# Small router products between key products, a narrower first wait for the query product, the sum's low part in four slices, and the shift row ahead of two stores

## The chip, the cores and the metric

One Trainium2 chip, one of its cores. The metric is the device time of one execution in microseconds. The kernel is written by hand: each engine (TensorE or PE, VectorE or DVE, ScalarE or ACT, GpSimd or POOL, and SyncE or SP, which only issues DMAs) has its own list of instructions in program order, and semaphores join the lists. An instruction that waits holds up everything behind it on its engine.

## The reference

Inputs are x (8 x 512 tokens x 512) and a context of 8 x 120 x 512. The first half is cross-attention with 16 heads of 32; all eight "experts" see the same attention output and their mean is taken, so that only the sum of the eight matrices We matters. The second half is a top-1 router over 8 experts, of which each takes 100 tokens at most, with one common matrix.

```
q = layernorm(x) @ Wq.T + bq;  k = ctx @ Wk.T + bk;  v = ctx @ Wv.T + bv
attn = softmax(q k.T / sqrt(32)) v                      # by head
x = x + tanh(g_xattn) * (mean_e(attn @ We[e].T + be[e]) @ Wo.T + bo)
h = layernorm(x); best = argmax(h @ w_gate)             # first 100 tokens of each expert
x = x + tanh(g_ffn) * gate * (h @ w_expert + b_expert)  # for those tokens
```

## The kernel before, in words

Every large product is split in two float16 parts, high and low, and made of three products (high by high, high by low, low by high), so each operand has a `_hi` and a `_lo` tile: ACT writes the high part out of a PSUM bank, then DVE writes the low part from the same bank and the high part.

**The prologue** is a list of 52 units, written down by `unit` and its callers. A unit is one PSUM bank: what PE does in it (`pe`), which semaphore counts PE waits for first (`needs`, and `free`: the evacuation of the unit eight places earlier, whose bank it takes), and what ACT and DVE do to empty it. PE, ACT and DVE each run through the list in its order. A unit's "done" is a count on `s_pa` (ACT) and on `s_pv` (DVE), and as both count along the list, a unit that waits for another also waits for all before that one. The units are: turning Wk (4 units), the biases, turning the context (one unit for each of 8 batch rows), four key units for batch rows 0 to 3 (`k_units(0)`), turning Wv (4), four key units for rows 4 to 7 (`k_units(1)`), turning Wq (4), the router's small units, turning Wo (4), and then the value products `v_unit(0)` to `v_unit(7)` with a few small units and the four units `x_unit` (which turn the first normalised x) between them. Key and value units have twelve products each. The small units are

- `gate_rows_unit` (L475): eight transposes of 4 x 128 out of `wg_rows`; it waits for `s_const`, which counts three loads, the last of them `bv_bc`; DVE copies it into `wg`;
- `be_unit` (L445): four products with the summed biases of the experts; it waits for `s_const` too;
- `gates_unit` (L469): one product that spreads the two gates, followed by the tanh on ACT;
- `gate_mean_unit` (L458): four products with `wg`; it needs DVE's copy of `wg`. After its evacuation DVE also makes `route_hi` and `route_lo` (L1299, L1302).

Beside the units ACT issues the DMAs that store the keys in a DRAM scratch (`store_k`, L1067; 12 for each half): those of the first half behind the unit four places after the last key unit of that half, those of the second half ahead of the unit `wogT`. DVE takes the statistics of the first x (`stats1`, `moments1`) behind the key unit ("k", 1, 2), and POOL makes 1/std from them and then adds up the eight matrices We in seven additions (`sum_we`), each of which waits for a load. SP has issued all loads in order; a load of We waits for the tile it overwrites.

**The first query product.** After the units PE goes through `run([-1], ...)`: the four query tiles of batch row 0 (`q_tile`, L892: `q_begin` and `q_end`), the router's product with x (`route_x`, L838), the products for the softmax maxima (`max_scores`, L896), and between them six late units (`mix_bias`, the four `("mix", k)` that multiply Wo with the sum of We, and `gateT`), which share three banks. `q_begin` calls `first_units_over` (L588) ahead of the first query product: all ACT and DVE evacuations of the 52 units, and all stores of the keys. The mix units need `sum_hi` (ACT, L1108) and `sum_lo` (DVE, `sum_low`, L1315: one instruction for 128 x 2048).

**Batch rows.** Then `run(range(0, B - 1), ...)` runs each batch row r with parts of rows r + 1 and r - 1 between its own. `scores(b, 0)` (L779) waits for `q_stack`, in which three parts are made by DMAs and the last partition holds the row of maxima, the "shift row": DVE `maxima`, PE `max_turn`, ACT `shift_row`, then a DMA on SP's queue into `q_stack`. On SP that DMA stands in the loop over r at L735 to L739; for r = 6 (B - 2) two stores of output tiles stand ahead of it:

```
                    if r == B - 2:
                        store_tiles(r, (0, 1))
                    e.wait_ge(s_sh, r + 2)
                    load(q_stack[3 * DK:STACK, :, :, :]..., shift[:, :], s_rsh)
```

The last batch row (7) has its own order with the experts' rows between.

Of the kernel before, what the change touches and what calls it, by code (L numbers as in the profile page):

```python
# [45 lines left out]
ALU = mybir.AluOpType  # L46
# [33 lines left out]
def build(nc, x, ctx, g_xattn, g_ffn, Wq, bq, Wk, bk, Wv, bv, We, be, Wo, bo, w_gate, w_expert, b_expert, out):  # L80
# [7 lines left out]
    with ExitStack() as st:  # L88
# [270 lines left out]
        def needs_of(*names):  # L359
            return [w for n in names for w in made[n]]  # L360
# [55 lines left out]
                ins = e.matmul(out_, a(pa, k), b(pb_, k), start=(i == 0), stop=(i == len(steps) - 1))  # L416
            return ins

        def k_units(half):
            lo_b, hi_b = half * HALF, (half + 1) * HALF  # L420
            for g in range(NK):
                def pe(e, b, g=g):
                    return products3(e, b[:, 0:HALF * SK],
                                     lambda p, k: (wkT_hi, wkT_lo)[p][:, k, g * P:(g + 1) * P],
                                     lambda p, k: (ctxT_hi, ctxT_lo)[p][:, k, lo_b * SK:hi_b * SK])
                unit(("k", half, g), pe,
                     needs_of(*[("wkT", k) for k in range(NK)], *[("ctxT", b_) for b_ in range(lo_b, hi_b)], "bias"),
                     act=lambda e, b, g=g: e.activation(
                         k_hi[:, lo_b:hi_b, g, :], b[:, 0:HALF * SK].rearrange("p (b s) -> p b s", s=SK),
                         ACT.Identity, bias=bias_cols[:, NK + g:NK + g + 1]),  # L430
                     dve=lambda e, b, g=g: e.scalar_tensor_tensor(
                         out=k_lo[:, lo_b:hi_b, g, :], in0=b[:, 0:HALF * SK].rearrange("p (b s) -> p b s", s=SK),
                         scalar=bias_cols[:, NK + g:NK + g + 1], in1=k_hi[:, lo_b:hi_b, g, :],
                         op0=ALU.add, op1=ALU.subtract))

        def v_unit(b_):
            def pe(e, b):
# [70 lines left out]
        def mix_units():  # L508
            def three(e, b, left, right):
                steps = [(o, i, j) for o in range(NK) for i, j in ((0, 0), (0, 1), (1, 0))]  # L510
                for n, (o, i, j) in enumerate(steps):
                    ins = e.matmul(b[:, :], left(i, o), right[j][:, o, :], start=(n == 0), stop=(n == len(steps) - 1))  # L512
                return ins

            wo = (woT_hi, woT_lo)
            unit("mix_bias", lambda e, b: three(e, b, lambda i, o: (be_hi, be_lo)[i][:, o:o + 1].to_broadcast([P, P]), wo),
                 needs_of("be_col", *[("woT", k) for k in range(NK)]) + [(s_bo, 16)],
                 dve=lambda e, b: e.scalar_tensor_tensor(out=mix_bias[:, :], in0=b[:, :],
                                                         scalar=1.0 / (BIAS_SCALE * OUT_SCALE), in1=bo_bc[:, :],
                                                         op0=ALU.mult, op1=ALU.add))  # L520
            for k in range(NK):
                def pe(e, b, k=k):
                    return three(e, b, lambda i, o: (sum_hi, sum_lo)[i][:, o, k * P:(k + 1) * P], wo)

                unit(("mix", k), pe, needs_of(*[("woT", o) for o in range(NK)]) + [(s_sumh, 1), (s_suml, 1)]
                     + ([(s_qhi, 3 + k), (s_qlo, 3 + k)] if k < 2 else []),
                     act=lambda e, b, k=k: e.activation(mixT_hi[:, k, :], b, ACT.Copy, scale=mix_scale[:, 0:1]),
                     dve=lambda e, b, k=k: e.scalar_tensor_tensor(
                         out=mixT_lo[:, k, :], in0=b, scalar=mix_scale[:, 0:1], in1=mixT_hi[:, k, :],
                         op0=ALU.mult, op1=ALU.subtract))  # L530
# [16 lines left out]
             dve=lambda e, b: e.tensor_tensor(bias_cols[:, :], b[:, 0:3 * NK], bias_unit[:, :], ALU.mult))  # L547
        for b_ in range(HALF + 2):
            ctx_unit(b_)
        k_units(0)  # L550
        for b_ in range(HALF + 2, B):
            ctx_unit(b_)
        weight_units("wvT", pair=(mixT_hi, mixT_lo), scale=V_SCALE)
        k_units(1)
        weight_units("wqT", pair=(wqT_hi, wqT_lo), scale=QK_SCALE)
        gate_rows_unit()
        be_unit()
        gates_unit()
        gate_mean_unit()
        weight_units("woT", pair=(woT_hi, woT_lo), scale=OUT_SCALE)  # L560
        v_unit(0)
        gate_out_rows_unit()
# [9 lines left out]
        N_FIRST = len(units)  # L572
        FIRST_ACT = sum(u["act"] is not None for u in units)
        FIRST_DVE = sum(u["dve"] is not None for u in units)
        late.append(N_FIRST)
        mix_units()
        gate_units()
# [64 lines left out]
        def _(e):  # L642
# [63 lines left out]
            for r in range(-1, B):  # L706
# [19 lines left out]
                if ok(r + 1):  # L726
                    e.wait_ge(s_sc, 4 * (r + 1))
                    e.wait_ge(s_qhi, 4 * (r + 2))
                    for part, src in ((0, q_hi), (2, q_hi), (1, q_lo)):
                        if part == 1:  # L730
                            e.wait_ge(s_qlo, 4 * (r + 2))
                        for j in range(HJ):
                            if (part, j) not in ACT_STACKS:
                                load(q_stack[part * DK:(part + 1) * DK, j, :, :], src[j * DK:(j + 1) * DK, :, :], s_rq)
                    if r == B - 2:  # L735
                        store_tiles(r, (0, 1))
                    e.wait_ge(s_sh, r + 2)
                    load(q_stack[3 * DK:STACK, :, :, :].rearrange("o j g s -> o (j g) s"),
                         shift[:, :], s_rsh)  # L739
                if ok(r + 2):  # L740
                    turn_x(r + 2)
            e.wait_ge(s_sc, 4 * B)
# [10 lines left out]
        def _(e):  # L753
# [82 lines left out]
                return ins  # L836

            def route_x(b, _):  # L838
                e.wait_ge(s_xth, 16 * b)
                e.wait_ge(s_xtl, 16 * b)  # L840
                if ok(b - 2):
# [25 lines left out]
            def q_begin(b, g):  # L867
                if g == 0:
                    if b == 0:
                        first_units_over(e)  # L870
                    e.wait_ge(s_xth, 16 * b)
                    e.wait_ge(s_xtl, 16 * b)
                    if ok(b - 2):
# [358 lines left out]
        def _(e):  # L1232
# [62 lines left out]
            for i in range(N_FIRST):  # L1295
                prepare(0, i)
                if units[i]["done"] == made["wg_mean"]:
# [4 lines left out]
                    e.scalar_tensor_tensor(out=route_lo[:, 0, :, 0:NE], in0=wgc[:, :, NE:2 * NE], scalar=GATE_SCALE,  # L1302
                                           in1=route_hi[:, 0, :, 0:NE], op0=ALU.mult,
                                           op1=ALU.subtract).then_inc(s_route, 1)
                if units[i]["done"] == made[("k", 1, 2)]:
                    for t in range(NT):
                        stats1(0, t)
                    moments1(0, 0)
# [3 lines left out]
                    moments1(1, 0)  # L1312
            first_units_over(e)

            def sum_low(_, __):  # L1315
                e.wait_ge(s_sumh, 1)
                e.scalar_tensor_tensor(out=sum_lo[:, :, :], in0=w_sum[:, :, :], scalar=SUM_SCALE, in1=sum_hi[:, :, :],
                                       op0=ALU.mult, op1=ALU.subtract).then_inc(s_suml, 1)

            def scale_bias(_, __):  # L1320
                e.wait_ge(*made["gates"][0])
# [155 lines left out]
            def add_table(b, _):  # L1477
# [5 lines left out]

            late_unit = lambda i: (prepare, 1, N_FIRST + i)
            run([-1], [
                (q_low, 1, 0), (maxima, 1, 0), (q_low, 1, 1), (sum_low, 1, 0), (q_low, 1, 2), (maxima, 1, 1),
                (q_low, 1, 3),
                (maxima, 1, 2), late_unit(0), (maxima, 1, 3),
                (normalise1, 2, 0), (normalise1, 2, 1), (normalise1, 2, 2), (normalise1, 2, 3),
                late_unit(1), (x_lo, 2, 0), (x_lo, 2, 1), late_unit(2), (x_lo, 2, 2), (x_lo, 2, 3), late_unit(3),  # L1490
                (scale_bias, 1, 0), late_unit(4),
            ])
# [276 lines left out]
```

## Time and profile before

| | us |
|---|---|
| three runs, median (lowest to highest) | 453.32 (452.45 to 453.39) |
| the profiled execution, its own time | 453.2 |
| its span, first to last instruction | 451.4 |
| PE busy | 427.3 (95%) |
| DVE busy | 343.1 (76%) |
| ACT busy | 224.3 (50%) |
| POOL busy | 161.9 (36%) |
| mean granted TensorE clock | 0.989 |

The span is 1.8 us shorter than the execution's time. Stretches on the timeline below are in us from the first instruction. A PE product's listed duration goes to its modelled end; in a run of products the distance of two starts is what each takes. The bracket behind a row is the idle time of the engine ahead of it, and what ended it. The granted clock is 1.00 at 2.4 GHz and 0.50 at 1.2 GHz. By time the prologue's units run to 75.8, batch row 0's own start to about 109, and each batch row takes 38.8 after that (the shift row is loaded at 298.31 and at 337.08).

### The profile page before, as it was taken

Reading aid. Unit: us, or ns where it says so; the run is one execution under the profiler, and the core shown is the slowest. Engines: PE = TensorE matmul, PEld = TensorE weight load, DVE = VectorE, ACT = ScalarE, POOL = GpSimd, SP = SyncE. Lnnn points to the kernel's source line nnn. Section 1 sums busy time; section 2 is a strip of 40 time slices with the busy share of each in tenths; the row PEclk is TensorE's granted clock in tenths of the full one; section 3 lists DMA queues with packets and bytes.
Section 4 is the critical chain, followed back from the end, with each engine's and each line's share of the span. In section 5 each row is a group of like instructions: output and inputs, shape, how many; then the busy total and the mean of one; then the engine's idle time right before and its main releaser. Section 6 shows DMA issues by size and latency. Waiting matters only on the chain.

```text
span 451.4 us, 8251 instructions
## 1 busy us (share of the span) xinstructions
PE 427.3 (95%) x2903; PEld 197.3 (44%) x2903; DVE 343.1 (76%) x671; ACT 224.3 (50%) x278; POOL 161.9 (36%) x149
## 2 busy tenths in 40 slices
PE   5998999899999999999999999999999998969996
PEld 4457565343344434534443443453444344324442
DVE  5438426786498889879889987988995598769983
ACT  4333321465753856476374656728456473657200
POOL 1005899206025308324430820523171062170460
PEclk9998899999999999999999999999999999989999
DMA  8997692058006724940780492188058016041683
GB/s 228 321 390 278 252 399 72 1 119 216 5 1 146 194 94 104 166 164 12 165 249 8 106 231 98 39 138 251 5 119 220 0 44 165 25 129 44 105 184 111
DMA packets 64842, 63.15 MB, mean 140 GB/s; under 512 B 41217, under 2 KB 44429, under 8 KB 64803
## 3 DMA queue, kind: packets, MB, share of 16 engines
q1 hardware_dynamic: 59691, 56.19, 46.8%
q0 software_dynamic: 1632, 3.49, 2.8%
q10 hardware_dynamic: 3480, 2.96, 1.9%
q8 instruction: 24, 0.39, 0.4%
q14 instruction: 15, 0.12, 0.1%
HBM read 29.59 MB, written 12.98 MB: 94 GB/s over the span
## 4 chain that ended last, share of the span: by engine, by line
PE 67%; DVE 12%; issue 10%; ACT 6%; DMA 3%; SPq 2%; DVEq 0%; ACTq 0%; POOLq 0%
PE ps L755 49%; PE ps L416 9%; ACT probs L1062 4%; DVE neg_max L1382 3%; DVE attn L1342 3%; PE ps L512 3%; PE ps L378 3%; DVE q_lo L1376 2%; SPq L644 2%; DMA raw<-in_L_xattn_Wk_dram 1%; DVE rden_both L1337 1%; DMA rows<-out_dram,row_ix 1%; PE ps L535 1%; PE ps L486 1%; DMA q_stack<-shift 1%
## 5 line engine op out<-in xcount | busy, mean ns | idle before, releaser
L1062 ACT ACTIVATE probs<-ps 120x2048 f32<-120x2048 f32 x32 | 60.1, 1879 | 43.7 <-PE ps L755 43.7
L1692 POOL TENSOR_TENSOR attn_lo<-attn,attn_hi 128x512 f16<-128x512 f32 x28 | 31.6, 1160 | 114.5 <-ACT attn_hi L1062 114.5
L1382 DVE TENSOR_REDUCE neg_max<-ps 128x16 f32<-128x1920 f32 x32 | 68.5, 2141 | 1.9 <-PE ps L755 1.9
L755 PE MATMUL ps<-xnT_hi,wqT_hi 128*128 128x512 f16 x128 | 48.6, 380 | 1.0 <-issue 0.9
L755 PE MATMUL ps<-mixT_hi,attn_hi 128*128 128x512 f16 x128 | 48.6, 380 | 0.0
L755 PE MATMUL ps<-mixT_lo,attn_hi 128*128 128x512 f16 x128 | 48.5, 379 | 0.0
L755 PE MATMUL ps<-xnT_lo,wqT_hi 128*128 128x512 f16 x128 | 48.5, 379 | 0.0
L1637 POOL TENSOR_SCALAR veps<-mv 128x4 f32<-128x4 f32 (+1 forms) x17 | 4.5, 265 | 121.5 <-DVE mv L1271 84.7
L1700 POOL TENSOR_TENSOR xb<-xb,mix_bias 128x512 f32<-128x512 f32 x32 | 39.6, 1269 | 22.5 <-DVE cb_col L1325 22.5
L1062 ACT ACTIVATE q_hi<-ps,bias_cols 128x512 f16<-128x512 f32 x32 | 21.9, 684 | 40.1 <-PE ps L755 40.1
L1376 DVE SCALAR_TENSOR_TENSOR q_lo<-ps,bias_cols,q_hi 128x512 f16<-128x512 f32 x32 | 23.8, 744 | 20.7 <-ACT q_hi L1062 20.7
L755 PE MATMUL ps<-q_stack,k_stack 97*120 97x512 f16 x128 | 33.9, 387 | 3.1 <-DMA q_stack<-shift 1.7
L755 PE MATMUL ps<-probs,den_sel 120*32 120x512 f32 x256 | 34.1, 605 | 0.1
L755 PE MATMUL ps<-probs,v_all 120*32 120x512 f32 x256 | 33.3, 592 | 0.7 <-ACT attn L1062 0.7
L755 PE MATMUL ps<-mixT_hi,attn_lo 128*128 128x512 f16 x128 | 33.0, 380 | 0.0
L755 PE MATMUL ps<-xnT_hi,wqT_lo 128*128 128x512 f16 x128 | 32.9, 379 | 0.0
L1062 ACT ACTIVATE q_stack<-q_hi 32x2048 f16<-32x2048 f16 x16 | 30.5, 1908 | 0.5
L1348 DVE SCALAR_TENSOR_TENSOR xb<-ps,xb 128x512 f32<-128x512 f32 x32 | 21.9, 685 | 11.2 <-PE ps L755 11.2
L1332 DVE RECIPROCAL rden<-ps 128x512 f32<-128x512 f32 x8 | 26.9, 3357 | 3.9 <-PE ps L755 3.9
L1062 ACT ACTIVATE attn<-ps 128x512 f32<-128x512 f32 x32 | 19.0, 594 | 17.4 <-PE ps L755 17.3
L1062 ACT ACTIVATE attn_hi<-attn 128x512 f16<-128x512 f32 x32 | 19.6, 630 | 12.5 <-DVE attn L1342 12.5
L755 PEld LDWEIGHTS ps<-q_stack,k_stack 97*120 97x120 f16 x128 | 15.0, 133 | 20.7 <-ACT probs L1062 7.9
(248 smaller groups left out, 822.8 us busy)
## 6 DMA issues: line engine op xcount, KB each, us to landing
xb<-in_x_dram SPq DMA_DIRECT2D x8, 1024.0 KB, 6.3
q_stack<-q_hi SPq DMA_DIRECT2D x48, 128.0 KB
out_dram<-xb SPq DMA_DIRECT2D x6, 1024.0 KB, 6.1
raw<-in_L_xattn_We_dram SPq DMA_DIRECT2D x5, 1024.0 KB, 11.5
q_stack<-q_lo SPq DMA_DIRECT2D x32, 128.0 KB
xb<-in_L_xattn_We_dram SPq DMA_DIRECT2D x3, 1024.0 KB, 11.2
k_stack<-k_scratch SPq DMA_DIRECT2D x8, 360.0 KB, 4.2
out_dram<-xb SPq DMA_DIRECT2D x8, 256.0 KB, 2.2
```

The lines of the kernel that those rows point to most:

```text
L378: ins = e.transpose(b[0:rows, i * cols:(i + 1) * cols], src_of(i), ident[0:cols, 0:cols])
L416: ins = e.matmul(out_, a(pa, k), b(pb_, k), start=(i == 0), stop=(i == len(steps) - 1))
L512: ins = e.matmul(b[:, :], left(i, o), right[j][:, o, :], start=(n == 0), stop=(n == len(steps) - 1))
L755: return e.matmul(out_, a, b, start=start, stop=stop, **kw)
L1062: return e.activation(out_, in_, func, **kw)
L1332: e.reciprocal(rden[:, :], den_b).then_inc(s_rec, 1)
L1342: e.tensor_tensor(attn[:, g, :], (den_b, num_b)[g % 2], attn[:, g, :], ALU.mult).then_inc(s_at, 1)
L1348: e.scalar_tensor_tensor(out=row, in0=pair_b[t % 2], scalar=1.0 / (ATTN_SCALE * MIX_SCALE), in1=row, op0=ALU.mult, op1=ALU.add).then_inc(s ...
L1376: e.scalar_tensor_tensor(out=q_lo[:, g, :], in0=pair_b[g % 2], scalar=bias_cols[:, g:g + 1], in1=q_hi[:, g, :], op0=ALU.add, op1=ALU.subtr ...
L1382: e.tensor_reduce(neg_max[:, :, :, g], quad[:, :, 0:NT * SK].rearrange("p j (t s) -> p t j s", t=NT), AX.X, ALU.max, negate=True).then_inc ...
L1692: e.tensor_tensor(attn_lo[:, g, :], attn[:, g, :], attn_hi[:, g, :], ALU.subtract).then_inc(s_alo, 1)
L1700: ins = e.tensor_tensor(row, row, mix_bias[:, :], ALU.add)
```

## The change

In the units: the context units 6 and 7 go between the first three key units of the first half; the small units go between the key units of the second half. DVE's statistics of x move from the third to the second key unit of that half. The sum's low part is made by 128 columns in four instructions, which stand later in DVE's list, and each mix unit waits for its own. PE's first query product waits for the units of Wq and x and for the last user of its bank (bank 7), and `first_units_over` moves to `route_x(0)`. On SP the shift row of r = 6 goes ahead of the two stores.

```diff
-        def k_units(half):
+        def k_units(half, between=()):
...
+                if g < len(between):
+                    between[g]()
...
-                unit(("mix", k), pe, needs_of(*[("woT", o) for o in range(NK)]) + [(s_sumh, 1), (s_suml, 1)]
+                unit(("mix", k), pe, needs_of(*[("woT", o) for o in range(NK)]) + [(s_sumh, 1), (s_suml, k + 1)]
...
-        k_units(0)
-        for b_ in range(HALF + 2, B):
-            ctx_unit(b_)
+        k_units(0, [lambda b_=b_: ctx_unit(b_) for b_ in range(HALF + 2, B)])
         weight_units("wvT", pair=(mixT_hi, mixT_lo), scale=V_SCALE)
-        k_units(1)
+
+        def gate_and_mean():
+            gates_unit()
+            gate_mean_unit()
+        k_units(1, [gate_rows_unit, be_unit, gate_and_mean])
         weight_units("wqT", pair=(wqT_hi, wqT_lo), scale=QK_SCALE)
-        gate_rows_unit()
-        be_unit()
-        gates_unit()
-        gate_mean_unit()
...
+        Q_BANK_DONE = next(u["done"] for u in reversed(units) if u["bank_no"] == 7)
...
-                    if r == B - 2:
-                        store_tiles(r, (0, 1))
                     e.wait_ge(s_sh, r + 2)
                     load(q_stack[3 * DK:STACK, :, :, :].rearrange("o j g s -> o (j g) s"),
                          shift[:, :], s_rsh)
+                    if r == B - 2:
+                        store_tiles(r, (0, 1))
...
             def route_x(b, _):
+                if b == 0:
+                    first_units_over(e)
...
             def q_begin(b, g):
                 if g == 0:
                     if b == 0:
-                        first_units_over(e)
+                        for s_, n in needs_of(*[("wqT", k) for k in range(NK)], *[("x", t) for t in range(NT)]) + Q_BANK_DONE:
+                            e.wait_ge(s_, n)
...
-                if units[i]["done"] == made[("k", 1, 2)]:
+                if units[i]["done"] == made[("k", 1, 1)]:
...
-            def sum_low(_, __):
+            def sum_low(_, k):
                 e.wait_ge(s_sumh, 1)
-                e.scalar_tensor_tensor(out=sum_lo[:, :, :], in0=w_sum[:, :, :], scalar=SUM_SCALE, in1=sum_hi[:, :, :],
-                                       op0=ALU.mult, op1=ALU.subtract).then_inc(s_suml, 1)
+                cols = slice(k * P, (k + 1) * P)
+                e.scalar_tensor_tensor(out=sum_lo[:, :, cols], in0=w_sum[:, :, cols], scalar=SUM_SCALE,
+                                       in1=sum_hi[:, :, cols], op0=ALU.mult, op1=ALU.subtract).then_inc(s_suml, 1)
...
-                (q_low, 1, 0), (maxima, 1, 0), (q_low, 1, 1), (sum_low, 1, 0), (q_low, 1, 2), (maxima, 1, 1),
-                (q_low, 1, 3),
-                (maxima, 1, 2), late_unit(0), (maxima, 1, 3),
-                (normalise1, 2, 0), (normalise1, 2, 1), (normalise1, 2, 2), (normalise1, 2, 3),
+                (q_low, 1, 0), (maxima, 1, 0), (q_low, 1, 1), (q_low, 1, 2), (maxima, 1, 1), (q_low, 1, 3),
+                (maxima, 1, 2), (sum_low, 1, 0), late_unit(0), (maxima, 1, 3), (sum_low, 1, 1), (sum_low, 1, 2),
+                (sum_low, 1, 3), (normalise1, 2, 0), (normalise1, 2, 1), (normalise1, 2, 2), (normalise1, 2, 3),
                 late_unit(1), (x_lo, 2, 0), (x_lo, 2, 1), late_unit(2), (x_lo, 2, 2), (x_lo, 2, 3), late_unit(3),
```

## Rows read from the trace of the kernel before

**Rows 1.** Windows: engines' busy us (count), granted clock, DMA share, GB/s

```profile
160.00:250.00 90.00, 89.14 (x682) 37.89 (x675) 80.85 (x152) 51.18 (x64) 31.04 (x30) 1.00 0.48 119
...
43.00:44.00 1.00, 1.00 (x7) 1.00 (x7) 0.00 (x0) 0.00 (x0) 1.00 (x1) 0.50 0.01 4
...
401.00:402.00 1.00, 0.84 (x5) 0.82 (x6) 1.00 (x3) 0.46 (x2) 0.69 (x2) 0.50 0.45 148
```

**Rows 2.** Timeline, PE, the second half's keys to the value units

```profile
27.38 0.36 PE L416 MATMUL ps<-ctxT_hi,wkT_hi 128*128 128x480 f16 x1 [0.54 <-DVE ctxT_lo L371]
...
37.09 1.91 PE L378 MATMUL ps<-ident,raw 128*128 128x128 f32 x16
38.94 1.04 PE L478 MATMUL ps<-ident,part_x 4*128 4x4 f32 x8
...
42.36 1.74 PE L461 MATMUL ps<-wg,ones_col 128*128 128x8 f32 x8 [1.27 <-DVE wg L481]
43.95 3.65 PE L378 MATMUL ps<-ident,xb 128*128 128x128 f32 x16
47.40 0.63 PE L416 MATMUL ps<-mixT_hi,ctxT_hi 128*120 128x512 f16 x1
...
51.05 3.60 PE L486 MATMUL ps<-xb,wgc 128*8 128x512 f32 x8
54.59 0.43 PE L416 MATMUL ps<-mixT_hi,ctxT_hi 128*120 128x512 f16 x1
```

**Rows 3.** Timeline, ACT, DVE and POOL beside the units; POOL's first and last of seven sums

```profile
32.39 1.08 ACT L370 ACTIVATE mixT_hi<-ps 128x512 f16<-128x512 f32 x2 [5.53 <-issue]
...
42.12 0.18 DVE L481 COPY wg<-ps 128x32 f32<-128x32 f32 x1
...
42.15 4.52 POOL L1673 TENSOR_TENSOR w_sum<-xb,raw 128x2048 f32<-128x2048 f32 x1
...
71.20 4.52 POOL L1673 TENSOR_TENSOR w_sum<-w_sum,xb 128x2048 f32<-128x2048 f32 x1
```

**Rows 4.** Timeline, DVE's evacuations of values and x, and PE's first query product

```profile
60.01 0.69 DVE L442 SCALAR_TENSOR_TENSOR v_all<-ps,bv_bc 120x512 f32<-120x512 f32 x1 [1.90 <-PE ps L416]
...
73.04 1.25 DVE L371 SCALAR_TENSOR_TENSOR xnT_lo<-ps,xnT_hi 128x512 f16<-128x512 f32 x2
...
75.83 0.69 DVE L442 SCALAR_TENSOR_TENSOR v_all<-ps,bv_bc 120x512 f32<-120x512 f32 x1 [0.94 <-PE ps L416]
...
76.72 0.38 PE L755 MATMUL ps<-xnT_hi,wqT_hi 128*128 128x512 f16 x1 [0.94 <-issue]
```

**Rows 5.** Timeline, DVE, PE and ACT, from the sum's low part to the first scores

```profile
85.15 2.28 DVE L1317 SCALAR_TENSOR_TENSOR sum_lo<-w_sum,sum_hi 128x2048 f16<-128x2048 f32 x1
...
90.30 0.39 PE L755 MATMUL ps<-k_hi,q_hi 32*128 32x120 f16 x16 [0.97 <-DVE neg_max L1382]
...
98.83 0.57 ACT L1062 ACTIVATE shift<-ps 16x512 f16<-16x512 f32 x1
...
102.62 1.03 PE L755 MATMUL ps<-q_stack,k_stack 97*120 97x512 f16 x4
```

**Rows 6.** Timeline, ACT, SP and PE, the shift row of the last batch row

```profile
375.24 0.59 ACT L1062 ACTIVATE shift<-ps 16x512 f16<-16x512 f32 x1 [1.74 <-issue]
...
375.41 1.07 SPq L644 DMA_DIRECT2D out_dram<-xb  x2
...
376.53 0.53 SPq L644 DMA_DIRECT2D q_stack<-shift  x1
...
378.27 0.38 PE L755 MATMUL ps<-mixT_lo,attn_hi 128*128 128x512 f16 x1
...
380.32 1.04 PE L755 MATMUL ps<-q_stack,k_stack 97*120 97x512 f16 x4 [1.67 <-DMA q_stack<-shift]
```

**Rows 7.** The tile `shift` over the whole span: its eight DMAs, issue to landing

```profile
DMA to landing us min/median/max: 2.1/2.1/3.4
```

**Rows 8.** DMA issues of the first 60 us: the four loads of Wo

```profile
xb<-in_L_xattn_Wo_dram SPq DMA_DIRECT2D x4, 256.0 KB, 10.9
```

## The prediction

> **What bounds the kernel now.** I read the windows first. Between 160 and 250 us PE is busy for 89.14 of 90 us and DVE for 80.85 [rows 1]: in the batch rows PE sets the pace, and DVE is near. So an early start of the batch rows is passed on to the end, and the question is what PE loses in the prologue and at the last batch row. The timeline of PE answers that. In the prologue it loses 0.54 us ahead of the second half's keys at 27.38, 1.27 us at 42.36, where the mean of the router's weights waits for DVE's copy of `wg`, and a stretch at the 1.2 GHz level: the granted clock is 0.50 at 43 us [rows 1, 2]. It fell after a stretch in which PE did only the small units (from 38.94) and then waited. Under it the 16 transposes of Wo take 3.45 us (43.95 to 47.40), where the 16 of Wq took 1.85 (37.09 to 38.94), and the first value unit takes 3.65 us (47.40 to 51.05) where a later one takes 2.59 (DVE's value evacuation at 60.01 comes 1.90 + 0.69 behind the one before) [rows 2, 4]. Last, the first query product starts at 76.72, 0.94 us after the last value product's modelled end, when the last value evacuation (75.83 to 76.52) is over [rows 4]. At the last batch row PE waits 1.67 us for the shift row [rows 6].
>
> **The change part by part.** *Context units between key units.* Nothing is added; 8 transposes move. The last low part of the context is then made long before 27.38, so the 0.54 us wait goes; returning from transposes to key products costs something once more. I take -0.5 (bounds -0.54 and 0). ACT's twelve DMA issues of the first half's keys now start behind the fourth turned Wv tile instead of within them (before, they held ACT idle for 5.53 us, until 32.39 [rows 3]). They take about 6.3 us (the idle time and what overlapped it); from about 27.5 on they let ACT go at about 33.8.
>
> *Small units between key units.* The key half takes 9.71 us (27.38 to 37.09), 2.43 a unit [rows 2]. The second half now starts at 26.9. The wait of 1.27 goes if DVE's copy of `wg` is there before PE comes to the mean. PE comes at 26.9 + three key units (7.3) + small units (42.36 - 1.27 - 38.94 = 2.15) = 36.3. The copy stands behind the first key unit's low part: ACT free at 33.8, high part about 0.7, low part about 0.7, copy 0.18 [rows 3]: 35.4. It fits with 0.9 us to spare. The wait: -1.27. The mean itself, 1.59 us (42.36 to 43.95) nearly all at the half clock, becomes about 0.9: -0.7. If the clock stays at 2.4 GHz, Wo's transposes give 3.45 - 1.85 = 1.60 and the first value unit 3.65 - 2.65 = 1.00 (2.59 and the change from transposes). I take it to stay: what came before the fall was 3.4 us of small units and waiting in one piece, and now no stretch of small products is then longer than about 1.1 us. Three returns to key products, whose waits PE's sequencer has to read, may show; I take +0.3 (bounds 0 and 1.4, the latter three times the 0.54 at 27.38, less 0.2). Sum: -1.27 - 0.7 - 1.6 - 1.0 + 0.3 = -4.3 (bounds -4.6 and, with the clock falling all the same, about -1.0). DVE's statistics come about 0.8 us earlier and with them POOL's seven sums (42.15 to 75.72 [rows 3]); they end at 75.0 to 75.7.
>
> *The first query product.* Its own operands are ready when DVE has the last two low parts of x (73.04 to 74.29), and its bank's last user (value unit 5) was emptied before that; only the evacuations of values 6 and 7 are no longer waited for [rows 4]. PE then follows the last value product at its pace: it could start at about 75.6 instead of 76.72. Some 20 waits stand in front of it, but all are satisfied while a value unit runs. I take -1.0 (bounds -1.1 and 0, if the sequencer's reading of waits is what is seen). `route_x(0)` has the wait now, 2.7 us later, when the evacuation (0.7 us) is over: 0.
>
> With these three PE's first query product starts about 5.8 us earlier, at 70.9. ACT then comes to the high part of We's sum at about 75.0, and the sum is ready by 75.7 at the latest. ACT's next high part of a query comes 3.0 us behind that, and the sum's takes 1.9: hidden, with about 0.4 us left on ACT and over 1 on PE.
>
> *The sum's low part.* Before, 2.28 us at 85.15 stood ahead of the second maxima, and PE waited 0.97 us for them at 90.30 [rows 5]. Taking it out frees only about 0.2 us, since the low and high parts of the third and fourth query tiles wait for PE anyway: -0.2. The slices are about 0.6 us each (2.28/4). The first lies in DVE's wait for `mix_bias`; three stand behind the last maxima, 1.8 us, ahead of the normalisations. Mix unit 0 needs slice 0 and has it; mix 1 needs slice 1 about when it is made (0.1 us to spare). What is late is the normalised x of batch row 1, about 1.6 us: ACT's `shift_row` stands behind two of its high parts, so it comes about 1.0 us later than 98.83 (counted from the first query product). The DMA then lands 2.1 us after its issue [rows 7] and PE's first scores (before at 102.62, without a wait [rows 5]) wait 0.4 us. Net of this part: +0.2 (bounds -0.2 and +1.0).
>
> *The shift row of the last batch row.* It was ready at 375.83 and was issued at 376.53 behind two stores; it took 3.4 us to land, against a median of 2.1 [rows 6, 7]. Now it is issued at about 375.87 and lands at 378.0, before PE is through with the product that starts at 378.27, so the scores follow at 378.6 instead of 380.32: -1.7 (bounds -1.9 and -0.7). The stores go out 0.6 us later; the gathers that need them wait for DVE's row index instead: 0.
> The Trainium skill, page "DMA: Bandwidth & Descriptors", section "Issuing engines are not separate DMA queues", has all transfers interleave on the same 16 engines. By that the stores just behind would still slow the row; were it 3.4 us again, the scores would start at about 379.6 and the gain would be 0.7.
>
> Sum: -0.5 - 4.3 - 1.0 + 0.2 - 1.7 = -7.3 us. From the profiled execution's 453.2 that is 445.9; that execution stands 0.1 us under the median of 453.32, so I leave it.
>
> **Rivals.**
> - *The clock falls all the same* somewhere between the keys and the value units. For: the whole of Wq's and Wo's transposes now stand together (3.7 us), and at 43 us the clock stayed low all through such transposes. Against: it was 1.00 through the long transposes of Wk and the context at the start. The terms 0.7, 1.6 and 1.0 go: about 449.2.
> - *The first query product's gap is not the wait*, so that this part of the change does nothing: the row calls it "issue". With the 0.3 for the returns at its bound too: about 448.
> - *The tail's clock.* At 401 the clock falls to 0.50 for about 3 us, behind a sparse stretch of PE [rows 1]. Everything is now over 7 us earlier; the fall could stay away (about -1.4, six products at 0.43 instead of 0.22: 444.5) or cost more (447). The Trainium skill, page "TensorE: Matmul & The Clock Gate", section "What's actually happening", says that the monitor looks at its own times and not at the kernel's; that is why both have a chance.
> - *The sum of We binds.* If the key stores, now 3.5 us earlier, slow the loads of We and POOL ends at 78 or later, ACT's queue is held and PE with it: 447 to 448.
> - *Slower: the constants come late.* `gate_rows_unit` waits for three loads, of which `bv_bc` was issued last, behind Wq. In this trace the unit first runs at 38.94 [rows 2], and nothing shows when the load landed. PE now comes to it at 29.3. If it landed as late as 38.9, PE would stand for 9.6 us, with a low clock behind it: about 453.2 - 7.3 + 9.6 = 455.5. The sign turns at a landing at 36.6. Against: the loads of Wo, issued after it, landed in a median of 10.9 us [rows 8], so about 24.
>
> **How the numbers follow.** Main case 0.62; clock falls 0.1; query gap stays 0.08; tail's clock 0.1; sum binds 0.05; constants late or something else that costs over 7 us 0.05. The forecast is 445.9. The main case with its bounds is 444.7 to 447.4; to take in most of the clock and gap cases the range goes from 443.9 to 449.2. About 0.2% (0.9 us, the spread of the three runs) is what a measurement of this kernel can tell from no change. Faster by more: 0.93; within: 0.03; slower: 0.04.
>
> **What would show it.** Right: no idle time ahead of the mean product, granted clock 1.00 from 42 to 50, the first value unit in 2.65 us and the second at about 49.8; the first query product at about 70.9, on the heels of the last value product; `shift` at the last batch row issued ahead of the stores and no wait for it; a small wait for the shift row at the first scores. Wrong: a wait of PE at `gate_rows_unit` or at the mean, a clock of 0.50 in the prologue, a wait of `sum_hi` on POOL that moves the second query tile, or new waits of PE on DVE among the batch rows that give the prologue's gain back.

## The result, and the profile after

The changed kernel takes 445.88 us (median of 5 runs, 444.54 to 447.92), the kernel before 452.45 beside it (5 runs, 451.42 to 453.39): ratio 0.9866, 95% interval 0.9829 to 0.9904. Run again later beside other kernels it took 445.99 (5 runs, 444.34 to 446.26), ratio 0.9818 (0.9781 to 0.9856). The forecast was 445.9.

| | before | after |
|---|---|---|
| profiled execution, own time, us | 453.2 | 444.54 |
| span, us | 451.4 | 442.8 |
| mean granted clock | 0.989 | 0.996 |
| PE busy, us | 427.3 (95%) | 423.2 (96%) |
| DVE busy, us | 343.1 | 340.7 |

The spans differ by 8.6 us, more than the forecast's 7.3, and 1.23 us of that is none of the change's: the first key product starts at 14.39 before and at 13.16 after, because the context's loads landed sooner (a median of 6.6 us after their issue instead of 7.5; the sixth at 12.10 instead of 13.32). The same start varied from 13.2 to 14.6 over the profiles of this study. So I count from the first key product on. Timeline of PE before, then of the changed kernel:

```profile
14.39 0.36 PE L416 MATMUL ps<-ctxT_hi,wkT_hi 128*128 128x480 f16 x1 [0.37 <-DVE ctxT_lo L371]
```

```profile
13.16 0.36 PE L416 MATMUL ps<-ctxT_hi,wkT_hi 128*128 128x480 f16 x1 [0.37 <-issue]
...
27.98 1.04 PE L480 MATMUL ps<-ident,part_x 4*128 4x4 f32 x8
31.48 1.05 PE L450 MATMUL ps<-ones_col,be_sb 8*128 8x1 f32 x8
34.99 0.38 PE L473 MATMUL ps<-gates,ones_col 1*128 1x2 f32 x2
35.30 1.06 PE L463 MATMUL ps<-wg,ones_col 128*128 128x8 f32 x8
38.64 1.91 PE L378 MATMUL ps<-ident,raw 128*128 128x128 f32 x16
40.39 1.91 PE L378 MATMUL ps<-ident,xb 128*128 128x128 f32 x16
42.13 0.38 PE L416 MATMUL ps<-mixT_hi,ctxT_hi 128*120 128x512 f16 x1
...
44.82 3.60 PE L488 MATMUL ps<-xb,wgc 128*8 128x512 f32 x8
48.35 0.43 PE L416 MATMUL ps<-mixT_hi,ctxT_hi 128*120 128x512 f16 x1
...
69.39 0.38 PE L756 MATMUL ps<-xnT_hi,wqT_hi 128*128 128x512 f16 x1
```

These rows answer to [rows 2] and to the last of [rows 4]. No bracket stands behind any row of the changed kernel here but the first: the wait of 1.27 us ahead of the mean, that of 0.54 ahead of the second half's keys and that of 0.94 ahead of the first query product are gone. Wo's 16 transposes take 1.74 us (40.39 to 42.13) instead of 3.45, and the first value unit 2.69 instead of 3.65. The windows show why; the clock column, third from the end, is 1.00 where it was 0.50 [rows 1]:

```profile
42.00:49.00 7.00, 7.00 (x26) 2.69 (x25) 3.71 (x7) 1.41 (x3) 6.51 (x2) 1.00 0.78 208
...
392.00:394.00 2.00, 1.44 (x6) 1.01 (x7) 1.61 (x3) 1.46 (x3) 1.70 (x2) 0.55 0.54 127
```

The second row is the tail, where the clock still falls for about 3 us. DVE's copy of `wg` ended 2.05 us ahead of the mean product, not 0.9: ACT was free of the key stores at 31.66, which is 18.5 us after the first key product, where the forecast had 19.4. And the sums on POOL ended before ACT asked for them:

```profile
33.07 0.18 DVE L483 COPY wg<-ps 128x32 f32<-128x32 f32 x1
...
69.06 4.53 POOL L1677 TENSOR_TENSOR w_sum<-w_sum,xb 128x2048 f32<-128x2048 f32 x1
...
73.62 1.91 ACT L1066 ACTIVATE sum_hi<-w_sum 128x2048 f16<-128x2048 f32 x1
```

Around the sum's low part and at the last shift row (answering to [rows 5] and [rows 6]):

```profile
82.70 0.39 PE L756 MATMUL ps<-k_hi,q_hi 32*128 32x120 f16 x16 [0.70 <-DVE neg_max L1387]
...
88.90 1.88 DVE L1322 SCALAR_TENSOR_TENSOR sum_lo<-w_sum,sum_hi 128x512 f16<-128x512 f32 x3
...
92.33 0.57 ACT L1066 ACTIVATE shift<-ps 16x512 f16<-16x512 f32 x1
...
95.37 1.04 PE L756 MATMUL ps<-q_stack,k_stack 97*120 97x512 f16 x4
...
368.62 0.52 SPq L645 DMA_DIRECT2D q_stack<-shift  x1
369.19 5.62 SPq L645 DMA_DIRECT2D out_dram<-xb  x4
371.82 1.04 PE L756 MATMUL ps<-q_stack,k_stack 97*120 97x512 f16 x4 [0.39 <-DMA q_stack<-shift]
```

Put together, in us after the first key product:

| | before | after | gained in the stretch |
|---|---|---|---|
| second value unit | 40.20 | 35.19 | 5.01 |
| first query product | 62.33 | 56.23 | 1.09 |
| first scores, batch row 0 | 88.23 | 82.21 | -0.08 |
| first scores, last batch row | 365.93 | 358.66 | 1.25 |
| end of the span | 437.01 | 429.64 | 0.10 |

The sum is 7.37 us. From batch row to batch row nothing was lost: of the 1.25 us in the fourth line, 1.28 are the last shift row's wait (1.67 before, 0.39 after).

### The profile page after: what moved, and what is told of

The parts are those of the page before. It is cut to its first block, busy times and chain, and to the rows that moved or that the text cites. A ratio compares the mean times of both kernels' runs of the same rounds, so it can differ in the third digit from the quotient of the medians.

```text
span 442.8 us, 8259 instructions
## 1 busy us (share of the span) xinstructions
PE 423.2 (96%) x2903; PEld 194.0 (44%) x2903; DVE 340.7 (77%) x674; ACT 223.6 (51%) x278; POOL 162.3 (37%) x149
## 4 chain that ended last, share of the span: by engine, by line
PE 70%; issue 11%; DVE 10%; ACT 6%; DMA 3%; SPq 0%; DVEq 0%; ACTq 0%; POOLq 0%
PE ps L756 51%; PE ps L416 9%; ACT probs L1066 4%; DVE neg_max L1387 3%; DVE attn L1347 3%; PE ps L378 3%; PE ps L514 3%; DVE q_lo L1381 2%; DMA raw<-in_L_xattn_Wk_dram 1%; DVE rden_both L1342 1%; DMA rows<-out_dram,row_ix 1%; PE ps L537 1%; PE ps L488 1%; PE ps L954 1%; DMA q_stack<-shift 1%
```

## The experiments

Each is the changed kernel with one edit, except where said. Times are medians, and each ratio is to the kernel before as it ran beside them (medians of 452.37 to 453.22). The changed kernel itself ran beside runs 3, 10 and 11 alone, and single executions of one kernel differ by over 3 us, so a difference of a microsecond between two medians of four runs shows little. What a part is worth is read from the profiles, in us after the first key product.

**1. Small units back in one piece behind Wq.**

```diff
-        k_units(1, [gate_rows_unit, be_unit, gate_and_mean])
+        k_units(1)
         weight_units("wqT", pair=(wqT_hi, wqT_lo), scale=QK_SCALE)
+        gate_rows_unit(); be_unit(); gate_and_mean()
...
-                if units[i]["done"] == made[("k", 1, 1)]:
+                if units[i]["done"] == made[("k", 1, 2)]:
```

> The changed kernel with the router's small units back in one piece behind Wq's transposes (and DVE's statistics back behind the third key unit). My theory (the wait for the copy of wg and the low clock behind the small units are what the move saves): PE waits about 1.3 us ahead of the mean product, the granted clock is 0.50 through Wo's transposes and part of the first value unit, and the second value unit starts 4.3 us later after the first key product than in the changed kernel (35.2 there, so 39.5): about 450 us. Rival (the gain came from earlier landings of the first loads, the clock falls or stays by chance): the second value unit at 35.2 to 37 us after the first key product, and a time within 1 us of the changed kernel's 445.9.

450.73 us (10 runs), ratio 0.9946 (0.9915 to 0.9978). The second value unit comes at 40.19. Timeline of PE and DVE, and a window:

```profile
42.27 0.18 DVE L483 COPY wg<-ps 128x32 f32<-128x32 f32 x1
```

```profile
42.51 1.77 PE L463 MATMUL ps<-wg,ones_col 128*128 128x8 f32 x8 [1.57 <-DVE wg L483]
44.13 3.65 PE L378 MATMUL ps<-ident,xb 128*128 128x128 f32 x16
```

```profile
44.00:45.00 1.00, 1.00 (x6) 1.00 (x6) 0.65 (x2) 0.00 (x0) 1.00 (x1) 0.50 0.00 1
```

The wait, the low clock and the long transposes are all back. The gain over the kernel before is 2.1 us by the medians, against 6.6 and 7.2 for the changed kernel: 4.5 to 5.1 us are lost. The theory held. One number is more than expected: 5.0 us at the second value unit, not 4.3. The context units still stood between keys here, and yet nothing of their gain was left: PE came earlier to the mean (the small units began at 24.24 instead of 24.55) and waited longer for DVE (1.57 instead of 1.27), whose copy of `wg` stood at 27.72, as before (27.73). That the gain needs the small units moved is shown in this one profile only, and it had a slow start: the first key unit took 2.81 us instead of 2.43, and ACT was held by the key stores until 19.41 instead of 18.50.

**2. Only `gate_rows_unit` between the keys**, the rest in one piece behind Wq.

```diff
-        k_units(1, [gate_rows_unit, be_unit, gate_and_mean])
+        k_units(1, [gate_rows_unit])
         weight_units("wqT", pair=(wqT_hi, wqT_lo), scale=QK_SCALE)
+        be_unit(); gate_and_mean()
```

> The changed kernel with only gate_rows_unit between key units; be_unit, the gates and the mean stand in one piece behind Wq's transposes (about 2 us of small products, with no wait in front of the mean). If the wait is needed for the clock to fall, the clock stays at 1.00 and the kernel is as fast as the changed one (second value unit 35.2 us after the first key product, 445.9). If 2 us of small products are enough, the clock falls: the second value unit comes 2.5 to 3.3 us later and the time is 448 to 449. I expect the clock to stay (0.65).

447.29 us (4 runs), ratio 0.9882 (0.9814 to 0.9949). PE's timeline has no idle time here, and still the clock fell:

```profile
38.15 1.05 PE L450 MATMUL ps<-ones_col,be_sb 8*128 8x1 f32 x8
39.06 0.36 PE L473 MATMUL ps<-gates,ones_col 1*128 1x2 f32 x2
39.35 1.06 PE L463 MATMUL ps<-wg,ones_col 128*128 128x8 f32 x8
40.26 3.57 PE L378 MATMUL ps<-ident,xb 128*128 128x128 f32 x16
```

```profile
39.00:40.00 1.00, 1.00 (x10) 0.98 (x9) 1.00 (x3) 0.46 (x3) 0.91 (x4) 1.00 0.95 348
40.00:41.00 1.00, 1.00 (x8) 1.00 (x8) 0.97 (x5) 0.00 (x0) 1.00 (x1) 0.69 1.00 363
41.00:42.00 1.00, 1.00 (x7) 1.00 (x6) 1.00 (x1) 0.60 (x1) 1.00 (x1) 0.50 0.50 180
```

The second value unit came 1.51 us late (36.70). My expectation that the clock would stay was wrong: no wait is needed for it to fall. The fall was cheaper than expected, since it caught only Wo's transposes: they took 3.36 us instead of 1.74, the mean had run before it, and the clock was back as the first value unit (43.62) began: 2.77 us instead of 2.69.

**3. The same 2 us piece, but between the third and the fourth key unit.**

```diff
-        k_units(1, [gate_rows_unit, be_unit, gate_and_mean])
+        k_units(1, [gate_rows_unit, lambda: None, three_small])   # be_unit, gates, mean
```

> The changed kernel with be_unit, the gates and the mean in one piece of 2 us between the third and the fourth key unit of the second half, so that dense key products stand on both sides of them. In the run with the same piece between Wq's and Wo's transposes the clock fell right behind it without any wait. If 2 us of small products alone make it fall, it falls here too (granted clock 0.50 behind the piece, second value unit 1 to 2 us later than 35.2 after the first key product). If it was the length of the whole stretch without key or value products (transposes, small products, transposes), the clock stays at 1.00 here and the second value unit comes at 35.2. I take the second (0.7).

445.36 us (4 runs, 444.97 to 445.53), ratio 0.9814 (0.9773 to 0.9855). The clock stayed:

```profile
34.73 1.05 PE L450 MATMUL ps<-ones_col,be_sb 8*128 8x1 f32 x8
35.64 0.36 PE L473 MATMUL ps<-gates,ones_col 1*128 1x2 f32 x2
35.93 1.06 PE L463 MATMUL ps<-wg,ones_col 128*128 128x8 f32 x8
39.27 1.91 PE L378 MATMUL ps<-ident,raw 128*128 128x128 f32 x16
```

```profile
38.00:40.00 2.00, 2.00 (x15) 1.36 (x13) 1.09 (x6) 0.53 (x1) 1.92 (x3) 1.00 1.07 394
40.00:44.00 4.00, 4.00 (x33) 3.56 (x32) 3.75 (x7) 4.00 (x9) 3.91 (x4) 1.00 0.57 204
```

Runs 2 and 3 have the same small products in the same length and differ in their neighbours: transposes on both sides, or dense key products. Only the first made the clock fall, in the one profile of each. The mean clocks, which the executions without a profile have too, point the same way: 0.989 to 0.992 over the four executions of run 2, 0.992 to 0.996 over the four of run 3. With one return to key products fewer, the second value unit came 0.19 us earlier (35.00) than in the changed kernel: a return costs about 0.2 us.

**4. `first_units_over` back ahead of the first query product.**

```diff
-                        for s_, n in needs_of(...) + Q_BANK_DONE:
-                            e.wait_ge(s_, n)
+                        first_units_over(e)
```

> The changed kernel with first_units_over back ahead of the first query product. My theory: a gap of about 1.1 us opens between the last value product and the first query product (it starts 57.3 us after the first key product instead of 56.2), and it is passed on to the end: 446.9 against 445.9. Rival (PE's sequencer reads about 20 waits either way): no difference in the gap.

447.83 us (4 runs, 446.04 to 448.95), ratio 0.9894 (0.9822 to 0.9966). The row of PE has its old bracket again:

```profile
71.35 0.38 PE L756 MATMUL ps<-xnT_hi,wqT_hi 128*128 128x512 f16 x1 [0.94 <-issue]
```

It comes at 57.33 instead of 56.23, and the first scores at 83.29 instead of 82.21: 1.1 us, passed on. The profile puts the time down to "issue", but it was the wait for the last evacuation.

**5. The last shift row behind the two stores again.**

```diff
+                    if r == B - 2:
+                        store_tiles(r, (0, 1))
                     e.wait_ge(s_sh, r + 2)
                     load(q_stack[3 * DK:STACK, ...], shift[:, :], s_rsh)
-                    if r == B - 2:
-                        store_tiles(r, (0, 1))
```

> The changed kernel with the last batch row's shift row behind the two stores again. My theory: it takes 3.4 us to land instead of 2.8, PE waits 1.67 us for it instead of 0.39, and the kernel is 1.3 us slower than the changed one: 447.2. Rival (the wait only moves, as ACT or DVE is late behind it): under 0.5 us.

447.25 us (4 runs, 445.70 to 448.91), ratio 0.9888 (0.9816 to 0.9961). Timeline of SP and PE:

```profile
367.53 1.22 SPq L645 DMA_DIRECT2D out_dram<-xb  x2
369.34 0.53 SPq L645 DMA_DIRECT2D q_stack<-shift  x1
```

```profile
372.96 1.04 PE L756 MATMUL ps<-q_stack,k_stack 97*120 97x512 f16 x4 [0.82 <-DMA q_stack<-shift]
```

Between the scores of batch row 0 and of the last one lie 276.89 us, against 276.45 in the changed kernel and 277.70 before. So the order is worth 0.4 us here and 1.25 in the pair above: in this profile PE waited 0.82 us with the stores ahead, in run 10, which has the old order too, 0.72, and in that of the kernel before 1.67. The expectation of 1.67 here was wrong. With the row ahead the waits were 0.45 or less in all profiles that have it.

**6. The two stores held until the third output tile is ready.**

```diff
                     if r == B - 2:
+                        e.wait_ge(s_x1, 4 * r + 3)
                         store_tiles(r, (0, 1))
```

> The changed kernel with the two stores behind the last shift row held until the third output tile is there, so that they start about 1.7 us later than the shift row. If the stores behind it are what makes it land in 2.8 us instead of 2.1, it lands in 2.1, PE's wait of 0.39 goes and the scores come 0.3 us earlier. If the q_stack loads ahead of it slow it, it still takes 2.8 us and nothing changes.

446.58 us (4 runs), ratio 0.9867 (0.9815 to 0.9919). The stores now start 1.8 us behind the row:

```profile
369.62 0.52 SPq L645 DMA_DIRECT2D q_stack<-shift  x1
371.46 1.33 SPq L645 DMA_DIRECT2D out_dram<-xb  x3
```

```profile
DMA to landing us min/median/max: 2.1/2.1/2.7
```

The longest landing of the eight shift rows is 2.7 us, where the changed kernel had 2.8 and, in run 12, 2.6. PE's scores stand at 358.48, as in the changed kernel's second profile (358.47, run 12). The prediction had weighed a rule of the Trainium skill (page "DMA: Bandwidth & Descriptors", section "Issuing engines are not separate DMA queues"), that transfers of all engines interleave, and with it that the stores behind would still slow the row. That the row takes more than 2.1 us fits transfers that interleave, but the stores behind are not what slows it.

The loads of `q_stack` are not either: they stand ahead of all eight shift rows, and the other seven land in 2.1 us. What only the last one has is the gather of rows of x that POOL issues 1.5 us (before, 2.2 us) earlier. In the changed kernel:

```profile
367.14 1.32 POOL L1720 DMA_INDIRECT rows<-in_x_dram,row_ix  x1 [0.20 <-issue]
```

It landed at 371.25, and the shift row at 371.46. In the 13 profiles other than that of the kernel before the row landed 0.17 to 0.21 us behind this gather, wherever the stores stood. In the profile of the kernel before the gather landed at 378.55 and the second store ahead of the row at 379.75, and the row at 379.97. So in each of the 14 the row landed about 0.2 us behind the later of the gather and the stores issued ahead of it. In run 5 the stores had gone out 1.8 and 0.95 us ahead of the row and had landed by 372.14, before the gather (372.44); in the kernel before they went out 1.1 and 0.5 us ahead. With that goes the difference between waits of 1.67 and 0.82 us. No run moved the gather, so that it sets the landing is read from the traces and not tested.

**7. The sum's low part in one instruction at its old place.**

```diff
-                (q_low, 1, 1), (q_low, 1, 2), ...  (maxima, 1, 2), (sum_low, 1, 0), late_unit(0), ...
+                (q_low, 1, 1), (sum_low, 1, 0), (q_low, 1, 2), ...  (maxima, 1, 2), late_unit(0), ...
```

> The changed kernel with the sum's low part in one instruction at its old place. My theory: the wait for the maxima goes from 0.70 back to 0.97 us and everything behind it is 0.2 us later up to the first scores, which is too little for the times to show; the shift row of batch row 0 comes about 1 us earlier without any use. If the slices cost more than they give (DVE later in batch row 1), this kernel is faster by up to 0.5 us instead.

446.65 us (4 runs, 444.86 to 448.75), ratio 0.9862 (0.9796 to 0.9928): not to be told from the changed kernel. From the first query product to the first scores lie 26.07 us, against 25.98 in the changed kernel and 25.90 before. The slices are worth nothing measurable. The profile has something else to show: its clock fell as the first key unit began, behind context transposes that had waited for their loads. That unit took 4.09 us instead of 2.43, and the second value unit came 1.66 us late (36.85).

```profile
12.00:14.00 2.00, 1.23 (x9) 0.84 (x10) 1.31 (x2) 1.16 (x3) 0.00 (x0) 0.97 1.09 262
14.00:16.00 2.00, 2.00 (x6) 0.73 (x6) 0.66 (x1) 0.14 (x1) 0.00 (x0) 0.50 1.04 311
```

That is no part of this edit; it is one reason why single runs of one kernel lie over 3 us apart.

**8. Context units 6 and 7 behind the first half's keys again** (`k_units(0)`, then the two `ctx_unit`).

> The changed kernel with context units 6 and 7 behind the first half's keys again. My theory: PE waits 0.5 us ahead of the second half's keys as in the kernel before, and the second value unit starts 35.7 us after the first key product instead of 35.2. The time differs by 0.5 us, which the runs hardly show. Rival (the wait is moved to ahead of the first value or query unit anyway): no difference at the second value unit.

446.62 us (4 runs), ratio 0.9876 (0.9823 to 0.9929). The wait of 0.54 us ahead of the second half's keys is back, and the second value unit comes at 35.88: 0.69 us later. The rival fell.

**9. The load of `bv_bc` behind those of Wo and the first x**, 2 MB later.

> The changed kernel with the load of bv_bc issued behind those of Wo and of the first x (2 MB more ahead of it). It tells how much room the first small unit has, which now waits for that load. If it landed early in the changed kernel, as I believe (first small unit 14.8 us after the first key product, without a wait), 2 MB at 350 GB/s are 5.7 us more: it would land at about 30 to 31 us from the start, PE would wait 2 to 4 us for it, and part of that would show in the time (447 to 450). If there is more room than that, nothing changes.

445.91 us (4 runs, 445.17 to 446.18), ratio 0.9855 (0.9803 to 0.9906). The first small unit starts at 14.82 as in the changed kernel, with no wait. The slower rival of the prediction had more than 2 MB of room.

**10. One part alone on the kernel before**: the small units between the second half's keys.

> The kernel before with one part of the change alone: the router's small units between the second half's key units (and DVE's statistics one key unit earlier). If the parts simply add, the second value unit comes 4.3 us earlier after the first key product than before (35.9 instead of 40.2), the rest is as before, and the time is 4.3 us under the kernel before. If the part needs the context units' move beside it, less.

The profiled execution agrees: the second value unit at 35.88, 4.32 us earlier, and 448.35 us. The median does not: 452.3 (10 runs), ratio 0.9976 (0.9943 to 1.0009). The runs fall in two groups: three with a mean clock of 0.992 at 448.4 to 449.7, the other seven with 0.980 or 0.985 at 451.5 to 455.2. A mean clock lower by 0.007 is some 6 us more at 1.2 GHz. Where these lie was not recorded, since the profile is of a run of the first group. Run 7 shows one place where the clock falls without the small units, the first key unit. But 6 us is also about the length of the fall in the prologue of the kernel before (from 42.5 to 49.4), so it is not excluded that this very fall came back in those seven runs. By the medians, then, the move alone is not shown to gain anything; that it gains 4.3 us is shown where the clock stays up. In the kernel with all parts no run went under 0.989. What of the other parts keeps the clock up stays open; no single one made it fall when undone (runs 4, 5, 7 and 8), though run 7 has two of four runs at 0.989 and 0.985.

**11. Fewer waits ahead of the late units, and the stores held**, as a try at a faster kernel.

```diff
-                 needs_of("be_col", *[("woT", k) for k in range(NK)]) + [(s_bo, 16)],
+                 [(s_bo, 16)],
...
-                unit(("mix", k), pe, needs_of(*[("woT", o) ...]) + [(s_sumh, 1), (s_suml, k + 1)]
+                unit(("mix", k), pe, [(s_suml, k + 1)]
...
                     if r == B - 2:
+                        e.wait_ge(s_x1, 4 * r + 3)
                         store_tiles(r, (0, 1))
```

> The changed kernel with two more edits: the late units no longer wait for evacuations that route_x(0) has already waited for (eight to ten waits fewer ahead of mix_bias and of each mix product), and the last two stores held as in the run before. If the 0.35 and 0.30 us of 'issue' ahead of these units are PE's sequencer reading waits, they shrink to about 0.1 each and the first scores come 0.3 to 0.5 us earlier: about 445.4 against 445.9. If they are something else, nothing changes.

446.25 us (5 runs, 445.02 to 446.55), ratio 0.9834 (0.9799 to 0.9869): no gain over the changed kernel's 445.99 beside it. The gaps did go: from the first query product to the first mix unit it is 16.83 us instead of 17.43. But the first scores now wait, and come at 82.06 instead of 82.21:

```profile
95.46 0.83 PE L757 MATMUL ps<-q_stack,k_stack 97*120 97x512 f16 x3 [0.38 <-DMA q_stack<-shift]
```

**12. The changed kernel again.**

> The changed kernel again, unchanged, beside the others on one chip. Its median should be 445.9 within 0.7 us, its milestones after the first key product within 0.1 us of those of its first profile (second value unit 35.2, first query product 56.2, first scores 82.2) except for the last shift row (0.4 to 0.9 us of waiting) and the tail's low clock (71.0 or 72.1 us from the last batch row's first scores to the end).

445.99 us (5 runs), ratio 0.9818 (0.9781 to 0.9856). Milestones 35.19, 56.23 and 82.22: those of the first profile within 0.01. PE waited 0.17 us at the last shift row, less than the 0.4 to 0.9 expected, and the tail took 71.86 us.

## Why the prediction was right

The forecast was 7.3 us and the runs gave 6.6 and, later, 7.2 (453.22 less 445.99); counted after the first key product the profile gives 7.37. That the medians met the forecast of 445.9 to 0.1 us is luck. The kernel before took 452.45 beside the first of them, where the forecast had started from 453.2, and the 7.37 of the profiles has 1.25 us for the shift row, which run 5 puts at 0.4. What each part cost when it was undone adds up to 6.6 us: 5.00 for the small units with the context units (run 1), 1.10 (run 4), 0.44 (run 5) and 0.09 (run 7).

- **Context units:** -0.5 forecast; 0.69 us when undone (run 8).
- **Small units:** -4.3 forecast for the wait, the mean, the transposes and the first value unit. Together with the context units 4.8 stood against 5.01 measured; alone 4.32 (run 10), in a profile whose clock stayed up. Wo's transposes gave 1.71 instead of 1.60, the value unit 0.96 instead of 1.00, the mean 0.68 instead of 0.7, the wait 1.27: 4.62 in all, of which the returns to the keys took 0.30 back, as forecast.
- **The clock** was given too much safety by its reason. I took it to stay because no piece of small products would be longer than 1.1 us. Run 3 shows 2.1 us of them among dense products without a fall, run 2 the same length between transposes with one. The neighbours count.
- **First query product:** -1.0 forecast; 1.09 in the pair, 1.10 undone (run 4).
- **The sum's low part:** +0.2 forecast; the stretch became 0.08 longer in the pair, and 0.09 longer still when the part was undone, so it is worth nothing either way. The step that was off is the wait of 0.4 us for the shift row of batch row 0. `shift_row` did start late, 22.94 us behind the first query product (92.33) against 22.11 before (98.83), but PE got there only at 25.98 and found it landed. The wait is real all the same: run 11 takes 0.6 us out ahead of it and gets 0.38 back as exactly this wait.
- **The last shift row:** -1.7 forecast, 1.25 in the pair, 0.4 in run 5. The direction was right and the size too large, for two reasons: the row took 2.8 us to land instead of 2.1, which goes with the gather ahead of it and not with the stores behind it (run 6), and of the three profiles with the old order that of the kernel before had by far the longest wait (1.67 against 0.82 and 0.72).
- **Range:** the prediction does not show how 444.7 to 447.4 follows for the main case. The parts' own bounds add up to 444.9 to 450.3, so its upper end was drawn tighter than its terms.
- **Rivals:** the sums on POOL ended early enough (73.59, with ACT there at 73.62, so only just); the constants had room (run 9); the query gap was the wait (run 4). The tail's clock falls in every profile, for about 3 us in five (71.0 to 71.2 us from the last batch row's first scores to the end) or about 7 in nine (71.9 to 72.3, and 71.5 in run 11): that rival's price was about 1 us. Both profiles of the pair have the short one.

One reading of the prediction was wrong and did no harm. Against a fall of the clock it held that the clock was at 1.00 through the long transposes of Wk and the context at the start. It was not, through Wk's and most of the context's. Eight transposes there take what 16 of Wq take (1.91, [rows 2]):

```profile
3.65 1.94 PE L378 MATMUL ps<-ident,raw 128*128 128x128 f32 x8 [3.65 <-DMA raw<-in_L_xattn_Wk_dram]
```

One took 0.42 us, as one of Wo's did under the granted clock of 0.50. The clock column says 1.00 up to 11.8 us because the trace's clock records begin only there. So the column can't be trusted at the start of a span, and the mean clock leaves that stretch out.

## What to carry to other kernels

Here small products cost more than their length when they stood in one piece beside transposes: spread between dense products they cost 0.1 to 0.2 us for each return, the latency of their evacuations was hidden, and no profile of that order shows a fall of the clock behind them. The seven low runs of run 10 leave open whether that order is enough by itself. Before a wait is widened to "everything so far", list what the next product truly reads. A part's gain is the gain only with its neighbours: the context units' move was worth 0.7 us with the small units moved and nothing in the one profile without. And one profile of a wait is one sample: the shift row's wait of 1.67 us was 0.82 and 0.72 in the two other profiles of the same order.

## What was not expected of the hardware

- The clock fell with PE never idle: 2.1 us of products with 1 to 8 columns between two rows of 16 fp32 transposes (run 2). The Trainium skill, page "TensorE: Matmul & The Clock Gate", section "HAM oscillation — how this bites in real kernels", tells of idle gaps; in that run there was none.
- An instruction of DVE on 128 x 32 elements took 2.35 us before (`route_hi`, 44.36 to 46.71, while POOL was in a sum from 42.15 to 46.67) and 0.18 us after (37.41), when POOL had only short instructions. In run 2 it took 3.62 us (40.84 to 44.46) under a sum from 39.89 to 44.43, and in run 1 2.31. Each time it ended within 0.1 us of the sum. PE waited for it in none of them. Timeline of DVE, before and after:

```profile
44.36 2.35 DVE L1299 TENSOR_SCALAR route_hi<-wgc 128x32 f16<-128x32 f32 x1
```

```profile
37.41 0.18 DVE L1303 TENSOR_SCALAR route_hi<-wgc 128x32 f16<-128x32 f32 x1
```
